# Second attention of a gated two-layer block on one core: scores in two PSUM banks, values in 32-column tiles, new orders

## The chip, the cores and the metric

One NeuronCore of a Trainium2 chip runs the whole program as one launch. The metric is device microseconds of an execution; the quoted time is the median of several executions. Engines are called TensorE (PE in rows, PEld its weight loads), VectorE (DVE), ScalarE (ACT), GpSimd (POOL) and SyncE (SP).

## The reference, cut to what matters

There are 16 batches of 256 tokens with 256 features, and a context of 120 rows for each batch.

```python
x = x + tanh(g_xattn[0]) * L0_xattn(layernorm(x), ctx, mask, ...)   # "A"
x = x + tanh(g_ffn[0])   * L0_ffn(layernorm(x), ...)                # "F", fp4-quantised, width 704
x = x + tanh(g_xattn[1]) * L1_xattn(layernorm(x), ctx, ctx, ...)    # "B"
x = x + tanh(g_ffn[1])   * L1_ffn(layernorm(x), ...)                # router "R" + experts "M"

# B: 16 heads of 16 features, all 120 context rows as keys and values
Q = (query @ Wq + bq); K = (key @ Wk + bk); V = (value @ Wv + bv)   # each split in 16 heads
attn = softmax(Q K^T / 4); ctx = attn @ V
return ctx @ Wo + bo
```

A is an attention of 4 heads of 64 features with one shared key and value head, rotary positions and a mask. R takes the two best of 8 experts per token (logits = x @ Wr + br). M runs the experts (width 1024) over the sorted tokens.

## The kernel before

**Two parts.** First a software pipeline over the 16 batches does A, F, B and the routing R, and splits the experts' weights in two fp16 parts (W). Then the expert phase M walks over tiles of sorted tokens; the change does not touch its code.

**Orders.** Each engine has a list in `ORDER` of stage/lag entries, which is worked through once in each step s, for batch s − lag. So in one steady step A of batch s, F of s − 1 (partly s − 2), and B and R of s − 3 (B's projections of s − 2) are interleaved on TensorE. A stage waits on semaphores for what it needs, so the order in a list decides what sits behind a wait. Steps run from s = −1 to 18; the steady ones take about 60 us.

**Numbers.** fp16 products are made of three matmuls (`three`, L1247 to L1249): high × high, low × high, high × low. Scores, transposes and values are fp32; an fp32 matmul that is no transpose shows as two records, each with a weight load of its own.

**B's rounds.** B has 8 rounds of 4 heads for each batch (2 halves `t` of 128 tokens × 4 rounds). Round k:
- B.s: TensorE writes scores of 4 heads (128 × 480) to `bank[3]` (L1319). It waits until the exponentials of round k − 1 have read that bank. VectorE takes the minimum of each head (L1008), ScalarE makes four exponentials to `b_ex[k % 2]` (L687).
- B.t: TensorE turns the four heads into `bank[4]` (L1332), ScalarE copies them to `b_pt` (L695).
- B.p: TensorE loads each head's turned probabilities as the stationary operand (120 × 128) and streams the head's values, 16 columns and one of ones (17 in all, L1343), into `bank[5]`. The 17th column is the sum of probabilities.
- After the last round of a half VectorE takes the reciprocal of the sums and multiplies (L1016, L1018).

After both halves B.ot turns the result (four transposes, L1359) into `bank[3]`, ScalarE copies the fp16 high part (L706), VectorE makes the low part (L972), and B.out multiplies by Wo, with the bias `bo` added by two one-row matmuls for each half (L1369, L1370). The key bias is also added by two one-row fp16 matmuls for each of four groups (L1431), the router's bias by one fp32 one-row matmul for each half (L1465).

**PSUM.** bank 0: A's turned input, half of A's queries, A's scores, A's turned output. bank 1: A's context, keys and values, turned probabilities, output. bank 2: the other half of A's rotary queries, then A's values. Bank 3, 4 and 5: B as above; B's queries use 3 and 5. Bank 5 also holds all of R, so B.q waits for `R.done`. Banks 6 and 7: F.

Of the kernel before, what the change touches and what calls it, by code (L numbers as in the profile page):

```python
# [34 lines left out]
QUAD = 4  # L35
WCH = 6
# [29 lines left out]
def gated_stack(nc, x, ctx, mask, g_x, g_f, rms_scale, q_w, kv_w, out_w, w_gate, w_up, w_down,  # L66
# [12 lines left out]
    with es:  # L79
# [25 lines left out]
        ones_h = sb("ones_h", [1, P], f16)  # L105
# [30 lines left out]
        bk_h = sb("bk_h", [1, 2, H1 * PITCH], f16)  # L136
        bvb = sb("bvb", [S, D])
        bo_h = sb("bo_h", [1, 2, D], f16)
        wr_s = sb("wr_s", [P, NK, NE])
        br_s = sb("br_s", [1, NE])  # L140
# [137 lines left out]
        class Signals:  # L278
# [12 lines left out]
         B.ot_mm, B.ot_hi, B.ot, B.out_mm, B.done, B.acc_out0, B.acc_out1) = (  # L291
            sem(f"b_{n}") for n in (
                "c_in0 c_in1 chain stats power rsqrt z zt ct zt_hi zt_lo ct_hi ct_lo q_mm k_mm q k v_mm v s_mm mn rd "
                "exp pt_mm pt pv_mm o ot_mm ot_hi ot out_mm done acc_out0 acc_out1").split())
# [22 lines left out]
        A.name, B.name = "A", "B"  # L317

# [31 lines left out]
        def over(ap, n):  # L350
# [7 lines left out]
            "SP": ("A.load/-1 B.out/3 B.load/0 W/0 R.rank/3").split(),  # L358
            "POOL": ("B.ln/2 R.ln/3 A.ln/-1 F.p0/1 W0/0 W1/0 F.p1/1 F.ln/0 W2/0 F.p/0 R.scatter/3").split(),
            "ACT": ("F.gu3/2 B.k/3 B.q/3 B.s0/3 B.s1/3 B.t0/3 F.ht0/2 B.s2/3 B.t1/3 B.t2/3 B.s3/3 F.ht1/2 A.s0/0 B.t3/3 "  # L360
                "B.s4/3 B.s5/3 B.t4/3 F.z/1 A.s1/0 A.t0/0 B.s6/3 B.t5/3 A.t1/0 B.s7/3 B.t6/3 B.t7/3 F.t/1 A.ot/0 B.ot/3 "
                "F.gu0/1 B.z/2 F.gu1/1 R.z/3 R.t/3 A.z/-1 B.ct/2 B.zt/2 F.gu2/1 A.t/-1 R.logit/3").split(),
# [291 lines left out]
        def _(act):  # L654
# [162 lines left out]
        def _(dve):  # L817
# [777 lines left out]
```

## Time and profile before

| | |
|---|---|
| median of 3 runs | 1848.67 us |
| fastest, slowest run | 1848.36, 1865.61 us |
| the profiled execution: its time | 1838.81 us |
| its span, first to last instruction | 1837.2 us |
| mean granted TensorE clock | 0.922 of full |

The profiled execution is 1.61 us longer than its span, and 9.86 us shorter than the median. In the profile's rows PE is a matmul, and its duration is not its distance to the next one: matmuls overlap, so the pace is read from one start to the next. A row of waits names the waiting engine and line, then what ended the wait.

### The profile page before, as it was taken

The page shows a single profiled execution, that of the slowest core. Times are in us where ns is not written, and L with a number is a line of the kernel's source. Part 1 is how long each engine was busy: PE and PEld are TensorE (multiplying, and loading weights), DVE is VectorE, ACT ScalarE, POOL GpSimd, SP SyncE. Part 2 cuts the span into 40 slices and gives each one's busy share as a digit, 9 for nine tenths or more (in the row PEclk, how much of TensorE's full clock was granted, in tenths as well). Part 3 has the DMA queues.
Part 4 walks back from the last instruction along what each step waited for, and adds up shares of the span by engine and source line. Part 5 has one row for each costly group of instructions (what it writes and reads, how often), then busy time and mean ns, then how long its engine had stood idle before and what let it go on. Part 6 is the DMA issues. An engine that isn't in the chain of part 4 may idle for free.

```text
span 1837.2 us, 35831 instructions
## 1 busy us (share of the span) xinstructions
PE 1540.0 (84%) x12221; PEld 1239.6 (67%) x12222; DVE 1121.2 (61%) x2782; ACT 886.8 (48%) x2169; POOL 591.9 (32%) x704
## 2 busy tenths in 40 slices
PE   2334899999998999899989877649999999999994
PEld 1223577667766767676766554438888888888884
DVE  4657678877787778787777552234444444444442
ACT  1111466656666656665655453214444544445542
POOL 0002324333434243334332421023443434434432
PEclk9557999999999999999999896569999999999998
DMA  5002211222022202221122000157213232232224
GB/s 172 11 0 78 81 57 37 92 92 84 10 92 92 91 9 87 92 93 43 51 84 84 7 7 12 48 160 239 39 32 100 34 103 34 33 101 34 29 34 114
DMA packets 63088, 123.60 MB, mean 67 GB/s; under 512 B 13890, under 2 KB 51899, under 8 KB 58811
## 3 DMA queue, kind: packets, MB, share of 16 engines
q1 hardware_dynamic: 45675, 102.75, 16.3%
q0 software_dynamic: 17312, 19.56, 6.6%
q8 instruction: 57, 0.93, 0.2%
q14 instruction: 44, 0.36, 0.1%
HBM read 78.63 MB, written 48.04 MB: 69 GB/s over the span
## 4 chain that ended last, share of the span: by engine, by line
PE 76%; DVE 9%; ACT 7%; issue 3%; DMA 2%; POOL 1%; SPq 0%; ACTq 0%; DVEq 0%; POOLq 0%
PE bank L1247 17%; PE bank L1249 16%; PE bank L1248 16%; PE bank L1319 9%; PE bank L1343 7%; PE bank L1332 3%; ACT b_ex L687 2%; DVE b_mn L1008 2%; ACT b_q L747 1%; PE bank L1359 1%; PE bank L1521 1%; ACT r_z L670 1%; PE bank L1467 1%; PE bank L1411 1%; PE bank L1431 1%
## 5 line engine op out<-in xcount | busy, mean ns | idle before, releaser
L1247 PE MATMUL bank<-split_room,wm 128*128 128x256 f16 x1152 | 314.9, 273 | 8.3 <-issue 6.9
L1249 PE MATMUL bank<-split_room,wm 128*128 128x256 f16 x1152 | 314.8, 273 | 0.0
L1248 PE MATMUL bank<-split_room,wm 128*128 128x256 f16 x1152 | 314.7, 273 | 0.0
L1224 DVE SCALAR_TENSOR_TENSOR split_room<-bank,b12e,split_room 128x256 f32<-128x256 f32 x288 | 138.3, 484 | 266.0 <-ACT split_room L798 258.2
L798 ACT ACTIVATE split_room<-bank,b12e 128x256 f32<-128x256 f32 x288 | 134.3, 470 | 196.0 <-PE bank L1249 192.6
L687 ACT ACTIVATE b_ex<-bank,b_mn 128x120 f32<-128x120 f32 x512 | 143.6, 373 | 117.5 <-DVE b_mn L1008 116.4
L1319 PE MATMUL bank<-b_k,b_q 128*128 128x480 f32 x256 | 140.8, 634 | 39.0 <-ACT b_ex L687 23.3
L1343 PEld LDWEIGHTS bank<-b_v,b_pt 120*128 120x128 f32 x1024 | 137.9, 204 | 36.0 <-issue 31.7
L643 POOL DMA_INDIRECT acc<-split_room,m_cur x72 | 115.3, 1602 | 131.7 <-ACT split_room L812 104.3
L1247 PE MATMUL bank<-wm,split_room 128*128 128x256 f16 x576 | 157.0, 273 | 0.0
L1249 PE MATMUL bank<-wm,split_room 128*128 128x256 f16 x576 | 157.0, 273 | 0.0
L1248 PE MATMUL bank<-wm,split_room 128*128 128x256 f16 x576 | 157.0, 273 | 0.0
L1008 DVE TENSOR_REDUCE b_mn<-bank 128x4 f32<-128x480 f32 x128 | 84.0, 656 | 95.1 <-PE bank L1319 91.8
L1343 PE MATMUL bank<-b_v,b_pt 120*128 120x17 f32 x1024 | 132.2, 265 | 0.9 <-DVE b_z L1018 0.9
L552 POOL TENSOR_TENSOR wm<-wm 128x704 f32<-128x704 f32 x32 | 53.5, 1672 | 245.8 <-DVE wm L1062 245.8
L1247 PEld LDWEIGHTS bank<-split_room,wm 128*128 128x128 f16 x1152 | 113.0, 98 | 23.8 <-issue 10.5
L806 ACT ACTIVATE split_room<-split_room 128x256 f16<-128x256 f32 x288 | 117.6, 408 | 19.8 <-DVE split_room L1224 18.0
L1249 PEld LDWEIGHTS bank<-split_room,wm 128*128 128x128 f16 x1152 | 113.0, 98 | 13.3
L1248 PEld LDWEIGHTS bank<-split_room,wm 128*128 128x128 f16 x1152 | 113.0, 98 | 13.2
L1235 DVE TENSOR_TENSOR split_room<-split_room 128x256 f16<-128x256 f32 x288 | 119.9, 416 | 2.2 <-ACT split_room L806 2.1
L695 ACT ACTIVATE b_pt<-bank 120x512 f32<-120x512 f32 x128 | 77.8, 608 | 74.1 <-PE bank L1332 74.0
L1332 PE MATMUL bank<-C,b_ex 128*120 128x128 f32 x512 | 83.8, 289 | 24.7 <-ACT b_pt L695 23.4
(358 smaller groups left out, 3859.7 us busy)
## 6 DMA issues: line engine op xcount, KB each, us to landing
split_room<-in_L_ffn_W SPq DMA_DIRECT2D x48, 512.0 KB, 8.4
wsplit<-split_room SPq DMA_DIRECT2D x16, 1536.0 KB, 6.5
wm<-wsplit SPq DMA_DIRECT2D x16, 1536.0 KB, 8.9
acc<-x SPq DMA_DIRECT2D x17, 256.0 KB, 2.1
xin<-in_x SPq DMA_DIRECT2D x16, 256.0 KB
rows<-r_row SPq DMA_DIRECT2D x16, 256.0 KB, 8.2
ct<-in_ctx SPq DMA_DIRECT2D x16, 120.0 KB
cb<-in_ctx SPq DMA_DIRECT2D x16, 120.0 KB, 2.1
```

Of the source, the lines that this page charges most:

```text
L687: last = act.activation(ex[:, k % 2, h], sb_[:, h * S:(h + 1) * S], ACT.Exp, bias=mn[:, k % 2, h:h + 1], scale=-1.0)
L798: act.activation(m_s[:, c % 2], bank[c % 4][:, 0:TILE], ACT.Silu, bias=b12e[:, p, 0, c:c + 1]).then_inc(M.silu, 1)
L806: act.activation(m_hh[:, 0, c], m_h[:, c % 3], ACT.Copy).then_inc(M.hi, 1)
L1008: dve.tensor_reduce(mn[:, k % 2], s4, AX.X, ALU.min).then_inc(G.mn, 1)
L1224: dve.scalar_tensor_tensor(m_h[:, c % 3], bank[c % 4][:, TILE:2 * TILE], b12e[:, p, 1, c:c + 1], m_s[:, c % 2], ALU.add, ALU.mult).then_in ...
L1235: dve.tensor_tensor(m_hh[:, 1, c], m_h[:, c % 3], m_hh[:, 0, c], ALU.subtract).then_inc(M.lo, 1)
L1247: pe.matmul(o, lh, rh, start=start, stop=False)
L1248: pe.matmul(o, ll, rh, start=False, stop=False)
L1249: return pe.matmul(o, lh, rl, start=False, stop=stop)
L1319: last = pe.matmul(sbk[:, at:at + side * S], q[:, c, t * P:(t + 1) * P], kk[:, c] if G is B else kk[:, :, :], start=G is B, stop=G is B or ...
L1332: last = pe.transpose(tbk[0:S, j * P:(j + 1) * P], ex[:, k % 2, j], ident)
L1343: last = pe.matmul(pbk[:, h * (width + 1):(h + 1) * (width + 1)], pt[:, k % 2, h - h0], v[:, h] if G is B else v[:, :], start=True, stop=True)
```

## The change

1. **A in two banks.** A.q is cut in A.q0 and A.q1 (a pair of heads each), each with its plain and its half-swapped product side by side, in bank 0 and in bank 1. The rotary stage on VectorE is cut in A.rk (keys and values), A.r0 and A.r1. A.q1 waits for `A.v`, since bank 1 held keys and values. A's values go to bank 0 (after the last exponentials) and bank 1. Bank 2 becomes free.
2. **B's scores in two banks by turns**, 3 and 2: B.s of round k waits for the exponentials of round k − 2. The exponentials now wait for the transposes of round k − 2, and for the reciprocal that reads the sums of the batch before. B's queries are made in banks 3 and 2, and B.q no longer waits for `R.done`; B.p of round 0 does.
3. **B's values stationary.** In B.p the values of a head (120 rows × 32 columns, 16 of them zeros) are the stationary operand, in one of four 32-column tiles, and the head's turned probabilities (120 × 128, fp32) stream. Two rounds accumulate in the same tiles. The result comes out turned already, 128 features × 128 tokens twice.
4. **Sums by accumulation.** Each exponential has an `accum_out`, the sum of its row. B.rx on VectorE takes the reciprocal of the 16 sums and spreads it over 256 columns (`b_rx`); TensorE turns that by two transposes at the end of B.p of each half, next to the values in bank 5. ScalarE copies it to SBUF (B.r), VectorE multiplies (B.p), ScalarE makes the high part (B.o), VectorE the low part (B.o). The stages B.ot, its four transposes among them, are gone, and B.out needs only the half it works on. The last transposes wait for B.rx.
5. **Biases.** bo and bk lie as high part in row 0 and low part in row 32 of a 33-row operand, and one matmul adds both. The router's bias is added by VectorE.
6. **Orders.** All five lists are new. On ScalarE R.logit (an exponential) moves from before the last gate activation F.gu3 to behind it. On TensorE R.rank moves behind B.q, F.ht0 moves from the end of a step to the next one's start, and B's rounds from t0 on belong to the next step. On SyncE the weights (W) come before B.out and B.load; on GpSimd W0 and W1 come before F.p0, and B.ln and R.ln are at the end. In preparation there are 8 DMAs more, and some memsets are larger.

```diff
-            "PE": ("F.ht1/2 A.s0/0 B.t3/3 B.s4/3 B.p2/3 A.s1/0 A.t0/0 B.s5/3 B.t4/3 F.d0/2 B.s6/3 B.p3/3 F.d1/2 B.p4/3 "
-                "B.t5/3 B.s7/3 A.t1/0 A.p0/0 B.t6/3 B.p5/3 A.p1/0 B.t7/3 F.t/1 B.p6/3 B.p7/3 A.ot/0 B.ot/3 F.gu0/1 "
-                "B.out/3 A.out/0 F.gu1/1 B.ct/2 B.zt/2 R.t/3 F.gu2/1 R.logit/3 A.t/-1 F.gu3/1 R.rank/3 B.k/2 B.q/2 "
-                "A.kv/-1 B.s0/2 B.v/2 A.q/-1 B.s1/2 B.t0/2 F.ht0/1 B.s2/2 B.p0/2 B.t1/2 B.t2/2 B.s3/2 B.p1/2").split(),
+            "SP": ("A.load/-1 W/0 B.out/3 B.load/0 R.rank/3").split(),
+            "POOL": ("A.ln/-1 W0/0 W1/0 F.p0/1 F.p1/1 F.ln/0 R.scatter/3 F.p/0 W2/0 B.ln/1 R.ln/2").split(),
+            "ACT": ("F.ht0/2 B.t2/3 B.s3/3 A.s0/0 F.ht1/2 B.t3/3 B.s4/3 B.s5/3 B.t4/3 B.s6/3 B.r3/3 F.z/1 A.s1/0 A.t0/0 "
+                "B.t5/3 A.t1/0 B.o0/3 B.s7/3 B.t6/3 F.t/1 B.t7/3 B.r7/3 B.o1/3 A.ot/0 F.gu0/1 B.z/2 F.gu1/1 R.z/3 R.t/3 "
+                "B.ct/2 A.z/-1 F.gu2/1 B.zt/2 A.t/-1 F.gu3/1 R.logit/3 B.k/2 B.q/2 B.s0/2 B.s1/2 B.t0/2 B.s2/2 B.t1/2").split(),
+            "DVE": ("A.rk/0 B.v/3 B.s1/3 F.q1b/2 B.s2/3 F.q1c/2 A.r0/0 A.r1/0 B.s3/3 F.ht0/2 A.s0/0 B.s4/3 F.ht1/2 B.s5/3 "
+                "F.ln/1 B.s6/3 B.rx0/3 W0/1 A.s1/0 B.p3/3 F.q/1 B.o0/3 B.s7/3 F.d1/2 W1/1 A.p0/0 A.p1/0 B.rx1/3 F.t/1 "
+                "W2/1 B.p7/3 B.ln/2 B.o1/3 A.ot/0 B.out/3 F.gu0/1 R.ln/3 A.out/0 A.ln/-1 F.gu1/1 F.q0a/1 B.ct/2 R.t/3 "
+                "F.gu2/1 B.zt/2 R.logit/3 A.t/-1 F.gu3/1 F.q0b/1 F.q1a/1 F.q0c/1 R.rank/3 B.s0/2").split(),
+            "PE": ("B.t0/3 B.s2/3 A.q1/0 B.p0/3 B.t1/3 F.ht0/2 B.t2/3 B.s3/3 B.p1/3 A.s0/0 F.ht1/2 B.t3/3 B.s4/3 B.p2/3 "
+                "B.s5/3 A.s1/0 B.t4/3 B.s6/3 A.t0/0 B.p3/3 F.d0/2 B.p4/3 B.t5/3 B.s7/3 A.t1/0 F.d1/2 B.t6/3 A.p0/0 A.p1/0 "
+                "F.t/1 B.p5/3 B.t7/3 A.ot/0 B.p6/3 B.p7/3 F.gu0/1 B.out/3 A.out/0 F.gu1/1 B.ct/2 B.zt/2 R.t/3 F.gu2/1 "
+                "A.t/-1 R.logit/3 F.gu3/1 B.k/2 B.q/2 R.rank/3 A.kv/-1 B.s0/2 B.v/2 B.s1/2 A.q0/-1").split(),
...
                         for h in range(QUAD):
-                            last = act.activation(ex[:, k % 2, h], sb_[:, h * S:(h + 1) * S], ACT.Exp,
-                                                  bias=mn[:, k % 2, h:h + 1], scale=-1.0)
+                            at = head_of(k % per, h)
+                            last = act.activation(ex[:, k % 2, h], sb_[:, h * S:(h + 1) * S], ACT.Exp, bias=mn[:, k % 2, h:h + 1], scale=-1.0,
+                                                  accum_out=b_sum[:, k // per, at:at + 1] if G is B else None)
...
+            def b_rx_(t):
+                def stage(b, p):
+                    dve.wait_ge(B.exp, b * RB + (t + 1) * (RB // NT))
+                    dve.reciprocal(b_rd[:, t], b_sum[:, t]).then_inc(B.rd, 1)
+                    if t or not isinstance(b, int) or b >= 1:
+                        held(dve, B.pv_mm, b * NT + t)
+                    dve.wait_ge(B.rd, b * NT + t + 1)
+                    dve.tensor_copy(b_rx[:, :, :].rearrange("p k (h d) -> p (k h) d", d=K1), over(b_rd[:, t], K1)).then_inc(B.rx, 1)
+                return stage
...
-                        else:
-                            pe.wait_ge(G.exp, b * n + k)
+                        elif k >= len(sbks):
+                            pe.wait_ge(G.exp, b * n + k + 1 - len(sbks))
+                        sbk = sbks[k % len(sbks)]
...
+                            r, c = k % per, k % per % 2
+                            for j in range(QUAD):
+                                at = r // 2 * (H1 // 2 * PITCH) + (4 * c + j) * PITCH
+                                last = pe.matmul(pbk[PITCH * j:PITCH * (j + 1), c * P:(c + 1) * P], v[:, at:at + PITCH], pt[:, k % 2, j],
+                                                 start=r == 0, stop=r == per - 1)
+                            if r == per - 1:
+                                pe.wait_ge(B.rx, b * NT + t + 1)
+                                for i in range(NK):
+                                    last = pe.transpose(pbk[:, D + i * P:D + (i + 1) * P], b_rx[:, i], ident)
...
-                    pe.matmul(o, ones_f[:, :], br_s[:, :], start=True, stop=False)
                     for k in range(NK):
-                        last = pe.matmul(o, r_zt[:, k, t * P:(t + 1) * P], wr_s[:, k], start=False, stop=k == NK - 1)
+                        last = pe.matmul(o, r_zt[:, k, t * P:(t + 1) * P], wr_s[:, k], start=k == 0, stop=k == NK - 1)
```

## Rows read from the trace of the kernel before

**Rows 1.** The page: busy time by engine, and the granted clock in 40 slices.

```profile
PE 1540.0 (84%) x12221; PEld 1239.6 (67%) x12222; DVE 1121.2 (61%) x2782; ACT 886.8 (48%) x2169; POOL 591.9 (32%) x704
...
PEclk9557999999999999999999896569999999999998
```

**Rows 2.** Stages: us, busy and count of each engine, clock, DMA share, GB/s.

```profile
461.60:521.40 59.80, 54.74 (x424) 41.77 (x422) 47.82 (x122) 37.52 (x92) 21.68 (x25) 1.00 0.20 69
521.40:582.50 61.10, 56.21 (x422) 42.19 (x420) 47.74 (x122) 37.43 (x92) 21.67 (x25) 0.97 0.21 72
1006.70:1069.80 63.10, 51.87 (x321) 36.97 (x321) 36.99 (x93) 31.94 (x75) 22.07 (x22) 0.86 0.03 10
1131.90:1176.00 44.10, 32.47 (x122) 23.52 (x122) 7.68 (x14) 15.52 (x45) 0.21 (x1) 0.63 0.00 1
1222.00:1837.00 615.00, 584.77 (x5472) 523.31 (x5470) 282.56 (x684) 280.59 (x697) 240.28 (x292) 0.98 0.31 73
```

**Rows 3.** TensorE's waits from 461.6 to 521.4: total us, times, longest.

```profile
PE bank L1332 <- ACT b_pt L695: 1.3, 1, 1.3
PE bank L1457 <- ACT r_z L670: 1.1, 1, 1.1
PE bank L1319 <- ACT b_q L747: 0.8, 1, 0.8
PE bank L1319 <- ACT b_ex L687: 0.8, 1, 0.8
PE bank L1359 <- DVE b_z L1018: 0.6, 1, 0.6
PE bank L1369 <- DVE b_zt L972: 0.4, 1, 0.4
```

**Rows 4.** Timeline of TensorE around the bias matmuls.

```profile
501.74 0.28 PE L1369 MATMUL bank<-bo_h,ones_h 1*128 1x256 f16 x1 [0.44 <-DVE b_zt L972]
501.86 0.27 PE L1370 MATMUL bank<-bo_h,ones_h 1*128 1x256 f16 x1
502.06 0.28 PE L1247 MATMUL bank<-wo,b_zt 128*128 128x256 f16 x1
502.17 0.27 PE L1248 MATMUL bank<-wo,b_zt 128*128 128x256 f16 x1
...
511.57 0.38 PE L1465 MATMUL bank<-br_s,ones_f 1*128 1x8 f32 x2
511.88 0.61 PE L1467 MATMUL bank<-wr_s,r_zt 128*128 128x8 f32 x4
```

**Rows 5.** Timeline of TensorE from 530 us: start, duration, operation.

```profile
530.64 1.07 PE L1319 MATMUL bank<-b_k,b_q 128*128 128x480 f32 x2 [1.04 <-ACT b_ex L687]
531.55 0.96 PE L1343 MATMUL bank<-b_v,b_pt 120*128 120x17 f32 x8
532.36 0.63 PE L1332 MATMUL bank<-C,b_ex 128*120 128x128 f32 x4
```

**Rows 6.** Timeline of VectorE: a minimum, rotary, and the second attention's division.

```profile
531.75 0.66 DVE L1008 TENSOR_REDUCE b_mn<-bank 128x4 f32<-128x480 f32 x1 [0.68 <-PE bank L1319]
...
533.32 0.67 DVE L987 TENSOR_TENSOR a_t<-bank,C 128x512 f32<-128x512 f32 x1
...
547.57 0.24 DVE L1016 RECIPROCAL b_rd<-bank 128x16 f32<-128x16 f32 x1
547.85 0.42 DVE L1018 TENSOR_TENSOR b_z<-bank,b_rd 128x256 f32<-128x256 f32 x1
```

**Rows 7.** Timeline of ScalarE: table loads, and a round of exponentials.

```profile
516.16 0.20 ACT L759 ACTIVATE r_e<-r_d 128x2 f32<-128x2 f32 x1
...
524.84 1.28 ACT L687 ACT_TABLE_LOAD   x1 [1.93 <-DVE b_mn L1008]
526.14 1.11 ACT L687 ACTIVATE b_ex<-bank,b_mn 128x120 f32<-128x120 f32 x4
```

**Rows 8.** Timeline of TensorE at the last batch's output.

```profile
1176.12 0.39 PE L1369 MATMUL bank<-bo_h,ones_h 1*128 1x256 f16 x1 [1.50 <-DVE b_zt L972]
```

More of the change, by code:

```diff
@@ L668, in stage @@
                         held(act, R.free, b + 2)
+                    if G is B and (not isinstance(b, int) or b >= 1):
+                        act.wait_ge(B.ot, b * NT)
                     for t in range(NT):
@@ L698, in rounds @@
                 return by_round(G, n, s=exps, t=turned)
-            ra = rounds(A, RA, a_ex, bank[0], a_mn, a_pt, bank[1])
-            rb = rounds(B, RB, b_ex, bank[3], b_mn, b_pt, bank[4])
+            ra = rounds(A, RA, a_ex, bank[0:1], a_mn, a_pt, bank[1])
+            rb = rounds(B, RB, b_ex, (bank[3], bank[2]), b_mn, b_pt, bank[4])
             def out_t(G, ot, bk):
@@ L999, in a_rotary, with stage, rounds @@
                 last.then_inc(A.k, 1)
-            def rounds(G, n, sbk, pbk, mn, rd, o, heads, width):
+            def a_rotary(c):
+                def stage(b, p):
+                    ca.go_on(b)
+                    dve.wait_ge(A.q_mm, b * 2 + c + 1)
+                    ca.link(dve.tensor_tensor(a_t1[:, c], bank[c][:, 0:T], C[:, C_CQ:C_CQ + T], ALU.mult))
+                    ca.link(dve.tensor_tensor(a_t2[:, c], bank[c][:, T:2 * T], C[:, C_SQ:C_SQ + T], ALU.mult))
+                    ca.wait()
+                    dve.tensor_tensor(a_q[:, c], a_t1[:, c], a_t2[:, c], ALU.add).then_inc(A.q, 1)
+                return stage
+            def rounds(G, n, sbks, pbks, mn, rd, o, heads, width):
                 per = n // NT
@@ L1339, in stage @@
                         pe.wait_ge(G.pt, b * n + k + 1)
-                        if t >= 1 and k % per == 0:
-                            pe.wait_ge(G.o, b * NT + t)
-                        for h in range(h0, h0 + QUAD):
-                            last = pe.matmul(pbk[:, h * (width + 1):(h + 1) * (width + 1)], pt[:, k % 2, h - h0],
-                                             v[:, h] if G is B else v[:, :], start=True, stop=True)
+                        pbk = pbks[t]
+                        if G is A and t == 0:
+                            pe.wait_ge(A.exp, b * n + n)
+                        if G is B and k == 0:
+                            pe.wait_ge(R.done, b + 1)
+                        if G is B and t >= 1 and k % per == 0:
+                            pe.wait_ge(G.o, b * NT + t)
+                        if G is A:
+                            for h in range(h0, h0 + QUAD):
+                                last = pe.matmul(pbk[:, h * (width + 1):(h + 1) * (width + 1)], pt[:, k % 2, h - h0],
+                                                 v[:, :], start=True, stop=True)
+                        else:
+                            r, c = k % per, k % per % 2
[7 more added lines that the diff above has]
+                                    last = pe.transpose(pbk[:, D + i * P:D + (i + 1) * P], b_rx[:, i], ident)
                         if k % per == per - 1:
@@ L1368, in stage @@
                         if bias is not None:
[L1369 to L1370 removed]
+                            pe.matmul(o, ones_h[:, :], bias[:, :], start=True, stop=False)
+                            pe.wait_ge(G.ot, b * NT + t + 1)
                         for k in range(NK):
@@ L1429, in b_k_ @@
                 for c in range(QUAD):
-                    for i in range(2):
-                        pe.matmul(bank[4][:, c * S:(c + 1) * S], bk_h[:, i, c * P:(c + 1) * P], ones_h[:, 0:S], start=i == 0, stop=False)
+                    pe.matmul(bank[4][:, c * S:(c + 1) * S], bk_h[:, c * P:(c + 1) * P], ones_h[:, 0:S], start=True, stop=False)
                     for k in range(NK):
```

165 lines of the change are left out of this document (98 added, 67 removed), and 3 rows, old and new, of the table ORDER.

## The prediction

> **What bounds the kernel now.** I read the page first: TensorE is busy 84% of the span, VectorE 61%, ScalarE 48% [rows 1]. The reader is to see that this is an average over two phases. In the digits of the granted clock the pipeline over batches stands at 9 (full speed) from the fifth slice to about the twenty-second, then falls to 6 and 5 before the expert phase brings it back [rows 1]. The table by stage gives sizes [rows 2]: a steady step takes 59.8 us, of which TensorE is busy 54.7, VectorE 47.8, ScalarE 37.5; one of the steps at 0.97 of the clock takes 61.1. The step at 1006.7, when A has run out, still takes 63.1 us at a clock of 0.86; the last B rounds take 44.1 us at 0.63; the experts 615.0 us, which the change leaves alone. So 1222 us can move, and in the steady part TensorE sets the pace: its work plus its waits. The view of waits of one step lists six, 1.3, 1.1, 0.8, 0.8, 0.6 and 0.4, together 5.0 us [rows 3]. TensorE's work is then 54.8 us, which agrees with its busy time. A change can help by work taken off TensorE or by waits that go; nothing else counts in the steady part.
>
> **The work on TensorE.**
> - *Router bias.* From the bias matmul's start to the next group is 0.31 us [rows 4], twice a step: −0.62.
> - *Output bias.* Two one-row matmuls start 0.12 apart [rows 4]; one of them goes in each half: −0.24. The key bias is half as wide (120 columns for 256), so 0.055 each, four times: −0.22.
> - *Transposes.* B.ot's four go, four of the reciprocals come, of the same shape: 0.
> - *Values.* Before, a round took from 531.55 to 532.36, 0.81 us [rows 5], eight weight loads of 128 columns with nearly nothing streamed. After, a round has four heads of two passes over 128 columns. The price of a pass: scores of 480 columns take 0.91 us in two passes (530.64 to 531.55 [rows 5]), so 0.455 × 128/480 = 0.12 us. No row shows column tiles at work together, so I bound it. Eight passes one after the other: 0.97 us. All four tiles side by side: two passes, 0.24. To either I add two changes of the tile shape. The only rows near it are those at the one-row bias: from it to the full array the starts are 0.20 apart where the next is 0.11 [rows 4], so about 0.09 a change, 0.18 a round. Range: 0.42 to 1.15 us a round, against 0.81. I take a value between: if the passes keep their order, the second pass of a head must wait for the first in its tile but can run with the next head's first, five pass times for eight: 0.60 + 0.18 = 0.78. So −0.03 × 8 rounds = −0.24 a step; ends −3.1 and +2.7.
>
> Sum of the work: −0.62 − 0.24 − 0.22 − 0.24 = −1.3 us a step.
>
> The Trainium skill's page "TensorEngine Tiling (Array Packing)", section "Theoretical Speedup", allows up to four times for columns of 32, but "Key Properties" says that a change of mode drains the array. By the first alone values would cost about what the lower end has; the second speaks against the change, and the wider start distance at the one-row bias [rows 4] looks like such a drain, though it is a row tile and no run here shows a column one.
>
> **The waits on TensorE.** I went through the new list of each engine with the durations of the rows: a round of scores 0.9 us [rows 5], a minimum 0.66 [rows 6], four exponentials 1.11 [rows 7].
> - *Waits that go.* The scores' wait for the exponentials (0.8, L1319 ← b_ex [rows 3]) goes with the second bank. The waits for B.z and B.zt (0.6 and 0.4 [rows 3]) go with B.ot: what follows the last values is ScalarE copy, VectorE multiply 0.42 [rows 6], high part, low part, about 1.8 us with hand-overs, behind a whole gate matmul group and the first half of B.out. −1.8 us.
> - *Waits that shrink.* B.t2 on the copy of t1 (1.3 [rows 3]) gets F.ht0 as cover, but now depends on the minimum of round 2, which stands behind a quantisation piece on VectorE: I leave 0.6, −0.7. B.s0's wait for B.q (0.8) gets R.rank as cover: −0.3. R.t's wait for R.z (1.1) has the same chain in both lists and stays.
> - *Waits that come.* A.s0 now stands earlier on TensorE, while VectorE first has a quantisation piece and then both rotary stages: six operations over 256 columns at the 0.42 of the multiply [rows 6] are 2.5 us where three over 512 were 2.0 (0.67 each [rows 6]): +0.9. The transposes at the end of B.p3 wait for B.rx, behind the minimum of round 6 on VectorE: reciprocal 0.24, spread about 0.4: +0.5. What is queued behind that is F.d0 and all after. B.t4 and B.p0, with less other work ahead of them: +0.5 and +0.3. Sum +2.2. Behind B.t4's wait stand B.s6 and the values.
> - *ScalarE's table loads.* Each is 1.28 us; one stands directly before the first exponentials of a batch [rows 7]. With R.logit behind F.gu3 the table of the exponentials stays, two loads for four. This takes 1.28 us out of the chain to B.t0 and is the reason that I add no wait there, although B.s0's minimum now stands behind R.rank's chain.
> - *Accumulated sums.* No row shows an exponential with accumulation. Bounds: free, or an extra instruction for each, at the 0.20 us of the smallest activation [rows 7], 0.8 a round. I take 0.05 for each, 0.2 a round, as the chain's instructions overlap; about two of the gates above feel it: +0.4.
>
> Waits: −1.8 − 1.0 + 2.2 + 0.4 = −0.2. With the work, −1.5 us a step. My walk ends more favourably where TensorE is later than its partners (its work is nowhere less than the rows say), and a wait that I count twice along one chain is paid once: four waits that come hang on one VectorE queue. I take 1.0 us off for that, estimated: −2.5 us a step, 57.3 for 59.8. VectorE then has 47.8 + about 1.3 (rotary 0.5, spreads 0.8) = 49.1 of 57.3.
>
> **The ends.** From 222.7 to 1006.7 us there are 13 steps: −33. The last 170 us before the experts are chains, not work. There the second bank lets scores run ahead, fewer table loads count in full, and B.ot's latency (a wait of 1.5 us on it at the end [rows 8], and its own transposes) goes: about −3 us for each of the three: −9. The preparation has eight DMAs more on SyncE, ahead of the first weights, and larger memsets; VectorE's preparation of B comes at step 2, long after: +1, between 0 and +4. W ahead of B.out on SyncE delays a store by four issues, which nothing needs for a step; W0 and W1 ahead of F.p0 on GpSimd run in time in which it stood idle. 0 for both. Sum −41: 1838.8 − 41 = 1797.8 for a profiled execution. The median stood 9.86 above the profiled one, so 1807.7; forecast 1808 us.
>
> **The rivals.**
> 1. *Column tiles side by side.* Then a round costs 0.42, −3.1 a step for −0.24: 2.9 × 16 = 46 us more: 1762. For it: the heads write four different groups of partitions. Against: fp32 needs two passes per head in order, and eight short instructions with a change of shape on both sides. The Trainium skill's page "TensorE: Matmul & The Clock Gate", section "Part 3: Packing small matmuls", reports 2.38 times for three column tiles; nothing in this trace bears on it.
> 2. *Column tiles one by one.* 1.15 for 0.78, 0.37 × 8 × 16 = 47 us: 1855, no change.
> 3. *The accumulators gate (slower).* If the sum costs an instruction of 0.20 to 0.28 us for each exponential, a round on ScalarE grows by 0.8 to 1.1 us, and ScalarE has 8 rounds in a step: +7 to +9 on 37.5 − 2.6. It is still under the step, but B.t0, B.p0, B.t2, B.t3, B.t4 and B.rx each stand close behind a round of exponentials. Six gates × 0.8 = 4.8, less 0.4 already counted: +4.4 × 16 = 70: 1878. It decides from about 0.15 us for each sum. For it: the waits of before behind ScalarE are half of all [rows 3]. Against: between gates the chain has slack.
> 4. *VectorE takes over.* It has 49 of 57; should the waits on it not overlap, my 1.0 us goes and the three ends give nothing: 1848.7 − 16 × 1.3 = 1828.
>
> **How the numbers follow.** A few runs of this kernel tell no change from one of 1%, 18.5 us. Chances: forecast (1785 to 1830) 0.42, rival 4 at its edge included in "faster" at 0.10; rival 1 0.20; rival 2 0.15; rival 3 0.13. Faster by over 1% (below 1830): 0.42 × 0.97 + 0.10 × 0.6 + 0.20 = 0.67; rival 2 lies within 1% for the most: same 0.18; slower 0.15. The range must reach rival 1 nearly and rival 2: 1755 to 1858, which leaves out rival 3 and some of rival 1, 0.2 in all.
>
> **What the profile would show.** Step length by the table of stages: 57.3. TensorE's rows at B.p: from the first of four heads to the next stage 0.78. Waits: no L1319 ← b_ex for B; A.s0 on the rotary 0.9; the reciprocal's transposes 0.5. Table loads 2 for 4 a step. The exponentials: 1.11 against 1.3. I am wrong if new waits on VectorE's queue at the start of a step exceed 2 us, if the clock falls below 0.97 in steady steps, or if a record of its own follows each exponential.

## The result, and the profile after

| | before | after |
|---|---|---|
| median of the runs | 1848.51 us (1834.79 to 1865.61) | 1753.41 us (1750.41 to 1754.71) |
| profiled execution: time, span | 1838.8, 1837.2 | 1752.59, 1751.0 |
| mean granted clock | 0.922 | 0.933 |

The changed kernel takes 0.951 of the time before (95% interval 0.945 to 0.956). The forecast was 1808 with a range from 1755: the direction was right, the gain of 95 us is more than twice the 41 that the sum gave, and the time lies just below the range.

The page's busy times, its granted clock in 40 slices and the head of its chain that ended last, of the kernel after, answer to [rows 1]:

```profile
PE 1444.2 (82%) x12061; PEld 1110.5 (63%) x12062; DVE 1150.0 (66%) x2878; ACT 910.7 (52%) x2701; POOL 595.4 (34%) x704
...
PEclk9556799999999999999999988599999999999997
...
PE 51%; DVE 28%; ACT 7%; issue 6%; POOL 5%; DMA 1%; SPq 0%; DVEq 0%; ACTq 0%; POOLq 0%
```

The head of the same chain in the kernel before:

```profile
PE 76%; DVE 9%; ACT 7%; issue 3%; DMA 2%; POOL 1%; SPq 0%; ACTq 0%; DVEq 0%; POOLq 0%
```

TensorE lost 96 us of busy time, VectorE gained 29. The two slices at 8 and the one at 5 after the pipeline stand where before had 8, 9, 6, 5, 6. VectorE's part of the chain rose from 9% to 28%.

Stages of the kernel after by windows (us, busy and count of each engine, clock, DMA share, GB/s): a steady step, the three stretches after A has run out, the experts. They answer to [rows 2].

```profile
446.50:502.70 56.20, 50.13 (x413) 34.63 (x411) 49.50 (x128) 38.71 (x125) 22.21 (x25) 1.00 0.23 76
952.20:1009.20 57.00, 42.99 (x311) 26.79 (x311) 39.33 (x97) 33.05 (x109) 18.44 (x20) 0.91 0.03 10
1009.20:1060.50 51.30, 36.94 (x259) 24.10 (x259) 23.21 (x68) 27.20 (x100) 12.29 (x14) 0.83 0.04 12
1060.50:1094.90 34.40, 22.04 (x136) 10.70 (x136) 9.80 (x29) 18.94 (x80) 3.91 (x4) 0.87 0.01 1
1136.00:1751.00 615.00, 584.76 (x5466) 523.05 (x5464) 282.41 (x684) 280.89 (x697) 241.38 (x292) 0.98 0.30 72
```

The two stretches of before whose like [rows 2] doesn't show, cut at the same events (the last one ends where VectorE begins to add B's output to the rows):

```profile
1069.80:1131.90 62.10, 44.52 (x269) 32.52 (x269) 23.28 (x67) 24.84 (x65) 16.35 (x18) 0.78 0.03 9
1131.90:1180.20 48.30, 36.39 (x138) 25.23 (x138) 7.74 (x14) 15.52 (x45) 0.21 (x1) 0.62 0.00 1
```

A step is the distance between two evictions of B's queries (`b_q`) on ScalarE. With it the 86.2 us of the span fall into three parts. The first eviction is at 222.6 us in one trace and at 222.7 in the other: the preparation cost nothing. The next 13 steps took 784.1 us and take 729.5: −54.6, where I had −33. From there to the first expert matmul it was 215.1 us and is 182.3: −32.8, where I had −9. The experts are 1.1 us longer. Not all of before's thirteen steps are at full clock; the next paragraph takes one that is.

In the steady step the two numbers that I had set up as work and waits can be read directly. TensorE's busy time went from 54.74 [rows 2] to 50.13: −4.6. Its waits are these (us in total, times, longest), against 5.0 in [rows 3]:

```profile
PE bank L1401 <- ACT b_ex L710: 1.7, 1, 1.7
PE bank L1541 <- ACT r_z L685: 1.1, 1, 1.1
PE bank L1384 <- DVE a_t L1037: 0.9, 1, 0.9
PE bank L1388 <- ACT b_q L782: 0.7, 1, 0.7
PE bank L1470 <- POOL f_z L567: 0.6, 1, 0.6
PE bank L1429 <- DVE b_rx L1073: 0.4, 1, 0.4
PE bank L1497 <- DVE f_ht L1159: 0.3, 1, 0.3
PE bank L1401 <- ACT b_pt L718: 0.2, 1, 0.2
```

They sum to 5.9, so +0.9. Work and waits give −3.7, the step −3.6. The reader should see that the waits did not shrink at all: they changed their places. In a step at full clock all of the gain is work.

Most of that work is the values. TensorE's timeline around two places of B.p in the kernel after, to be read against the middle row of [rows 5]:

```profile
480.08 0.43 PE L1424 MATMUL bank<-b_pt,b_v 120*32 120x128 f32 x8
480.43 0.65 PE L1401 MATMUL bank<-C,b_ex 128*120 128x128 f32 x4
...
481.45 0.83 PE L1424 MATMUL bank<-b_pt,b_v 120*32 120x128 f32 x16
482.21 0.44 PE L1429 MATMUL bank<-C,b_rx 128*128 128x128 f32 x2
```

From start to the next start one round takes 0.35 us, and two take 0.76, where one took 0.81: 0.45 × 8 = −3.6 a step. The trace's single records show how: in the round at 480.08 four of the eight matmuls start within 0.02 us, and the other four, again within 0.02 us, begin 0.13 us after the first. Before, the eight of a round start 0.11 apart. With the −1.1 of the bias terms that is −4.7, and the busy time shows −4.6.

### The profile page after: what moved, and what is told of

Its sections match the earlier page's. It is cut to its first block, busy times and chain, and to the rows that moved or that the text cites. A ratio compares the mean times of both kernels' runs of the same rounds, so it can differ in the third digit from the quotient of the medians.

```text
span 1751.0 us, 36348 instructions
## 1 busy us (share of the span) xinstructions
PE 1444.2 (82%) x12061; PEld 1110.5 (63%) x12062; DVE 1150.0 (66%) x2878; ACT 910.7 (52%) x2701; POOL 595.4 (34%) x704
## 4 chain that ended last, share of the span: by engine, by line
PE 51%; DVE 28%; ACT 7%; issue 6%; POOL 5%; DMA 1%; SPq 0%; DVEq 0%; ACTq 0%; POOLq 0%
PE bank L1312 13%; PE bank L1314 13%; PE bank L1313 13%; PE bank L1388 3%; DVE b_mn L1047 2%; ACT b_ex L710 2%; POOL f_z L567 2%; PE bank L1401 2%; DVE wm L1125 1%; POOL f_z L565 1%; DVE wm L1117 1%; DVE r_pick L1219 1%; PE bank L1424 1%; DVE a_t L1037 1%; POOL slots L595 1%
## 5 line engine op out<-in xcount | busy, mean ns | idle before, releaser
L710 ACT ACTIVATE b_ex<-bank,b_mn 128x120 f32<-128x120 f32 x512 | 177.4, 360 | 130.0 <-DVE b_mn L1047 121.1
L1388 PE MATMUL bank<-b_k,b_q 128*128 128x480 f32 x256 | 129.1, 586 | 13.9 <-ACT b_q L782 13.9
L1047 DVE TENSOR_REDUCE b_mn<-bank 128x4 f32<-128x480 f32 x128 | 83.3, 651 | 59.8 <-PE bank L1388 53.7
L710 ACT ACTIVATION_READ_ACCUMULATOR b_ex<-bank,b_mn 128x1 f32 x512 | 104.4, 204 | 0.0
L1401 PEld LDWEIGHTS bank<-C,b_ex 128*120 128x120 f32 x512 | 56.1, 140 | 68.4 <-ACT b_ex L710 45.3
L625 POOL DMA_INDIRECT split_room<-rows,m_next x76 | 75.0, 987 | 43.2 <-POOL m_next L622 31.8
```

The lines of the kernel that those rows point to most:

```text
L710: last = act.activation(ex[:, k % 2, h], sb_[:, h * S:(h + 1) * S], ACT.Exp, bias=mn[:, k % 2, h:h + 1], scale=-1.0, accum_out=b_sum[:, k ...
L1047: dve.tensor_reduce(mn[:, k % 2], s4, AX.X, ALU.min).then_inc(G.mn, 1)
L1388: last = pe.matmul(sbk[:, at:at + side * S], q[:, c, t * P:(t + 1) * P], kk[:, c] if G is B else kk[:, :, :], start=G is B, stop=G is B or ...
L1401: last = pe.transpose(tbk[0:S, j * P:(j + 1) * P], ex[:, k % 2, j], ident)
```

## The experiments

After this result my theory was: values in column tiles run side by side (rival 1) and that is the steady gain; the two banks keep TensorE from standing still, and so keep its clock, in the ends. Rivals: the orders alone carry the gain; the sums still cost something; a wait on VectorE can be had back by a better order. "Step" is the mean of the first 12 steps, "rest" the time from the last of them to the first expert matmul, both from one profile; "before" is the median of the kernel before on the same chip.

| kernel | median, us | ratio to before (95%) | before | step | rest |
|---|---|---|---|---|---|
| before | 1848.5 | | | 60.0 | 279.0 |
| after | 1753.4 | 0.951 (0.945 to 0.956) | 1848.5 | 56.2 | 238.0 |
| one_tile | 1783.3 | 0.963 (0.959 to 0.967) | 1854.5 | 58.5 | 245.1 |
| one_bank | 1891.9 | 1.022 (1.017 to 1.026) | 1854.5 | 64.6 | 275.3 |
| no_sums | 1770.8 | 0.956 (0.952 to 0.960) | 1854.5 | 56.8 | |
| old_orders | 1875.1 | 1.013 (1.008 to 1.018) | 1854.5 | 64.3 | 259.3 |
| one_bank_busy | 1852.9 | 1.013 (1.008 to 1.018) | 1828.1 | 62.1 | 265.6 |
| tables_back | 1812.7 | 0.991 (0.987 to 0.995) | 1828.1 | 59.9 | 254.1 |
| rank_later | 1754.2 | 0.959 (0.955 to 0.963) | 1828.1 | 56.2 | |
| before_bias | 1835.7 | 1.003 (1.000 to 1.007) | 1828.1 | 60.0 | |
| before_busy | 1851.3 | 1.000 (0.997 to 1.004) | 1850.3 | | |
| after_busy | 1766.8 | 0.957 (0.951 to 0.963) | 1850.3 | | |
| v_first | 1757.2 | 0.952 (0.946 to 0.958) | 1850.3 | 56.2 | |
| rotary_first | 1783.7 | 0.973 (0.970 to 0.976) | 1829.9 | 58.0 | |

The kernel before differs by 1.4% from chip to chip (1828 to 1854), and its gain with it: rank_later, within 1 us of after, is 74 us under the before of its chip, where after is 95 under its own. After itself ran on one chip only. On three others rank_later (1754.2), v_first (1757.2) and no_sums (1770.8, of which 16.4 are longer experts, as told below) stand within 4 us of it, so I compare variants of after by their own medians and steps, and use the ratio for the sign. The steps of before come from a profile on the first chip; beside a variant from another chip they are a weaker measure.

**one_tile: the four heads of a round in one column tile.** Each head gets its round's tile; four heads overwrite two column ranges in turn, so the values are not those of the reference; count and shape of the instructions stay.

```
-  last = pe.matmul(pbk[PITCH * j:PITCH * (j + 1), c * P:(c + 1) * P], v[:, at:at + PITCH], pt[:, k % 2, j],
-                   start=r == 0, stop=r == per - 1)
+  last = pe.matmul(pbk[PITCH * r:PITCH * (r + 1), j % 2 * P:(j % 2 + 1) * P], v[:, at:at + PITCH], pt[:, k % 2, j],
+                   start=j == 0, stop=j == QUAD - 1)
```

> The kernel after, but the four heads of a round of B.p all go to one 32-column tile (round r to tile r), so that they can't run side by side; the tile shape, the 32-column weight loads and all orders stay (the values of B come out wrong, so its result is not the reference's). Theory, overlap: the after-rows show a round of B.p in 0.35 us from start to start where eight passes of 128 columns one after the other would be 8 x 0.11 = 0.9 us; so +0.5 x 8 x 16 = +64 us, about 1817 us. Rival, weight loads: the gain in B.p came from the loads (32 columns for 128), and tiles don't matter: within 10 us of 1753.

TensorE's timeline in one_tile, the same places as above:

```profile
488.52 1.06 PE L1424 MATMUL bank<-b_pt,b_v 120*32 120x128 f32 x8
489.51 0.65 PE L1401 MATMUL bank<-C,b_ex 128*120 128x128 f32 x4
...
490.76 1.53 PE L1424 MATMUL bank<-b_pt,b_v 120*32 120x128 f32 x16
492.22 0.44 PE L1429 MATMUL bank<-C,b_rx 128*128 128x128 f32 x2
```

A round takes 0.99, or 0.73 where two stand together (these two lie in two different tiles), for 0.35 and 0.38: the tiles do run side by side, both passes of fp32 included, and the 32-column weight loads, which one_tile has too, don't explain it. 0.99 is my upper end without the change of shape (0.97). TensorE's busy time in a step rises by 4.5 us (50.1 to 54.6), as the rounds add (six times 0.64 and twice 0.35), but the kernel lost only 2.3 us a step: the waits for A's rotary, for `f_z`, for `b_rx` and for `f_ht` are gone, 2.2 us of them, because TensorE now comes later than VectorE. The theory on tiles holds; its price in time is reduced by waits that were behind it. The time it expected, 1817, was 34 us too high for the same reason.

**one_bank: B's scores in one bank again.**

```
-            rb = rounds(B, RB, b_ex, (bank[3], bank[2]), b_mn, b_pt, bank[4])
+            rb = rounds(B, RB, b_ex, (bank[3],), b_mn, b_pt, bank[4])
```

(and so in the two other engines' programs)

> The kernel after, but B's scores use bank 3 alone, so that round k waits for the exponentials of round k-1 again; all orders stay. Theory, overlap of tiles carries the steady steps and the second bank mainly the ends: +1 us a step and +10 at the ends, about 1780 us. Rival, the second bank carries the change: +3 us a step and more, over 1805 us.

It is slower than the kernel before, and 112 us above what the theory expected. The largest wait of a step from 482 us, then TensorE's timeline behind it, and the window of that stretch:

```profile
PE bank L1388 <- ACT b_ex L710: 5.8, 2, 3.8
```

```profile
486.82 1.97 PE L1388 MATMUL bank<-b_k,b_q 128*128 128x480 f32 x2 [3.78 <-ACT b_ex L710]
488.59 0.42 PE L1312 MATMUL bank<-a_zt,wqa 128*128 128x256 f16 x1
488.80 0.42 PE L1313 MATMUL bank<-a_zt,wqa 128*128 128x256 f16 x1
```

```profile
486.80:492.00 5.20, 5.17 (x18) 3.38 (x19) 1.99 (x3) 1.48 (x8) 0.00 (x0) 0.50 0.00 0
482.00:547.00 65.00, 54.89 (x410) 37.38 (x409) 49.86 (x130) 39.11 (x124) 21.69 (x27) 0.92 0.20 65
```

In the list of after, only B.v stands between B.s0 and B.s1; with one bank B.s1 needs the exponentials of round 0 to be done, 3.8 us. Behind this wait the granted clock is 0.50: fp16 matmuls of 256 columns start 0.21 apart, 1.2 GHz, where they start 0.11 apart in after, 2.4 GHz. The step has 5.8 − 1.7 = 4.1 us more waits, and 54.9 for 50.1 = 4.8 us more busy time for the same instructions. So half of the 8.4 us is a wait and half the clock that it takes away.

**one_bank_busy: matmuls in front of these waits.** one_bank, with matmuls into the bank that nothing else uses:

```
                         elif k >= len(sbks):
+                            if G is B and k in (1, 5):
+                                for _ in range(24 if k == 1 else 10):
+                                    pe.matmul(bank[2][:, 0:D], wo1[:, 0, 0, 0:P], wo1[:, 0, 1], start=True, stop=True)
```

> The kernel with scores in one bank (1891.9 us), and on TensorE, right before the waits of B.s1 and B.s5 for the exponentials, 24 and 10 extra fp16 matmuls of 256 columns (0.11 us each) into bank 2, whose results nobody reads. Nothing is taken away and both waits end when they did. Theory, the clock: the wait of 3.8 us before B.s1 is followed by 5 us of rows at half speed (matmuls 0.21 apart for 0.11), so work put into the wait keeps the clock: about 2.5 us a step less, 1850 us. Rival: the clock there follows from something else: 1892 us or more by what the extra work costs.

A step of it by windows:

```profile
482.00:544.00 62.00, 54.40 (x443) 37.83 (x442) 49.98 (x127) 38.79 (x124) 21.95 (x25) 1.00 0.21 69
```

Against the row of one_bank above TensorE has 33 more records and 0.5 us less busy time, and the clock is at 1.00. The 34 added matmuls are 3.7 us of work at full clock and stand in the waits, so the clock gave back about 4.2 us a step, near the 4.8 above; the step is 2.5 us shorter. That the clock is a cost of its own is shown. The kernel's median is 39 us lower, but the two ran on different chips; by the ratios to before it is 0.8%, some 16 us.

**no_sums: exponentials without accumulation.** The sums are a constant, so B's softmax is not normalised.

```
-  last = act.activation(ex[:, k % 2, h], sb_[:, h * S:(h + 1) * S], ACT.Exp, bias=mn[:, k % 2, h:h + 1], scale=-1.0,
-                        accum_out=b_sum[:, k // per, at:at + 1] if G is B else None)
+  last = act.activation(ex[:, k % 2, h], sb_[:, h * S:(h + 1) * S], ACT.Exp, bias=mn[:, k % 2, h:h + 1], scale=-1.0)
```

> The kernel after without accum_out: the exponentials don't sum, the sums are a constant set once (the softmax of B is not normalised rightly). The rows after show the exponentials 0.34 apart and a read of the accumulator for each, where they were 0.25 apart before: 0.37 us a round on ScalarE. Theory: only the wait before B.t0 and the last chain of rounds feel it, -0.4 us a step, -10 us in all, about 1743. Rival (the prediction's third): six gates in a step feel it, -2.2 us a step, -35 us or more.

ScalarE's timeline in after shows what was taken away:

```profile
399.94 0.36 ACT L710 ACTIVATE b_ex<-bank,b_mn 128x120 f32<-128x120 f32 x1
400.20 0.19 ACT L710 ACTIVATION_READ_ACCUMULATOR b_ex<-bank,b_mn 128x1 f32 x1
400.29 0.35 ACT L710 ACTIVATE b_ex<-bank,b_mn 128x120 f32<-128x120 f32 x1
```

Each exponential is followed by a record of 0.20 us, which is rival 3's instruction, but the exponentials start 0.34 apart for 0.25: 0.09 more each, 0.37 a round. Without it nothing is gained: the start of the experts is 1138.6 against 1134.5, and the wait before B.t0 is 1.6 for 1.7. It now ends on VectorE's `b_v` and not on the exponentials, so VectorE's queue hides what the sums cost there. The median is 17 us longer because the phase of the experts takes 632.9 us for 616.5; wrong values of B send the rows to the experts otherwise, which I take for the reason. It says nothing on the sums. Rival 3 fell: the instruction is there and costs nothing in this kernel.

**old_orders: the changed code with the lists of before.** B.r, B.rx and A.rk, which before doesn't have, are put in where their inputs are there. TensorE's list begins as before's:

```
-            "PE": ("B.t0/3 B.s2/3 A.q1/0 B.p0/3 B.t1/3 F.ht0/2 B.t2/3 B.s3/3 B.p1/3 A.s0/0 F.ht1/2 B.t3/3 B.s4/3 B.p2/3 "
+            "PE": ("F.ht1/2 A.s0/0 B.t3/3 B.s4/3 B.p2/3 A.s1/0 A.t0/0 B.s5/3 B.t4/3 F.d0/2 B.s6/3 B.p3/3 F.d1/2 B.p4/3 "
...
```

> The kernel after with the five order lists of the kernel before, the new stages put in where their partners stood (B.rx behind the minimum of its half's round 6 or behind A.p1, B.r and B.o at B.ot's and B.p's places, A.rk at the end of a step on VectorE). Theory, the operations carry the change: work on TensorE is 4.5 us a step less whatever the order, so most of the gain stays, 1775 to 1800 us. Rival, the orders carry it: 1830 us or more.

1.3% slower than before, though TensorE has 4.6 us less to do in a step. Its largest waits from 472 to 538 us:

```profile
PE bank L1401 <- ACT b_pt L718: 3.2, 2, 1.7
PE bank L1401 <- ACT b_ex L710: 2.8, 1, 2.8
PE bank L1312 <- DVE wm L1148: 1.7, 2, 1.0
```

With the smaller ones they are 11.0 us for 5.9, and the clock is 0.90 to 0.95 in the steps but the first. The theory's 1775 to 1800 missed, the rival's 1830 or more holds: work taken from TensorE counts only if the lists let the partners follow.

**tables_back: one entry of ScalarE's list.**

```
-                "... A.t/-1 F.gu3/1 R.logit/3 B.k/2 B.q/2 B.s0/2 B.s1/2 B.t0/2 B.s2/2 B.t1/2").split(),
+                "... A.t/-1 R.logit/3 F.gu3/1 B.k/2 B.q/2 B.s0/2 B.s1/2 B.t0/2 B.s2/2 B.t1/2").split(),
```

> The kernel after with R.logit on ScalarE back in front of the last gate activation, as in the kernel before: four table loads a step for two. Theory: the load of 1.28 us stands again between the minimum and the first exponential, before which TensorE waits already: +1.2 us a step, about 1772. Rival: ScalarE is idle there for 4 us and takes the load meanwhile: within 3 us of 1753.

The table loads on ScalarE from 480 to 540 us, and TensorE's largest wait there:

```profile
501.00 1.28 ACT L751 ACT_TABLE_LOAD   x1
513.16 1.28 ACT L794 ACT_TABLE_LOAD   x1 [0.74 <-DVE r_d L1198]
514.67 1.28 ACT L751 ACT_TABLE_LOAD   x1
526.10 1.28 ACT L710 ACT_TABLE_LOAD   x1 [5.53 <-DVE b_mn L1047]
```

```profile
PE bank L1401 <- ACT b_ex L710: 4.5, 1, 4.5
```

Four loads for two. The last stands in the chain to B.t0, whose wait grows from 1.7 to 4.5. As A.s0's wait is gone, the waits of a step grow only by 1.8 in sum; the step grows by 3.7, with TensorE busy for some 2 us more, and its clock is 0.94 to 0.97. Without this one entry the kernel is 59 us slower, also against rank_later on the same chip. I had expected 19: again a load was priced by its duration and not by what a longer wait does to the clock.

**rank_later, v_first, rotary_first: the waits on VectorE.** The first two put R.rank's chain behind B.s0, and behind B.v too; the third puts A's rotary before a piece of the experts' quantisation, and F.ht1 two entries later.

```
-  rank_later:   F.q0c/1 R.rank/3 B.s0/2      v_first: A.rk/0 B.v/3 B.s1/3           rotary_first: F.q1c/2 A.r0/0 A.r1/0 B.s3/3
+                F.q0c/1 B.s0/2 R.rank/3               A.rk/0 B.s1/3                               A.r0/0 A.r1/0 F.q1c/2 B.s3/3
+                                                      F.q0c/1 B.s0/2 B.v/2 R.rank/3
```

> The kernel after with one entry moved on VectorE: R.rank behind B.s0 instead of before it. In the rows after, R.rank's chain takes 4.1 us there (it took 1.7 before), because two of its operations last until a GpSimd operation that runs beside them ends (1.59 and 1.16 us), and the minimum of round 0 stands behind it; TensorE then waits 1.7 us before B.t0. Theory: that wait goes, about 1.2 us a step, 1735 us. Rival: the keys' stage A.rk and the minimum of round 1 come as much later, and the wait moves to A.q1 or B.t1: within 5 us of 1753.

> The kernel after with VectorE's order B.s0, B.v, R.rank, A.rk where it is R.rank, B.s0, A.rk, B.v. With R.rank alone behind B.s0 the wait before B.t0 stayed at 1.5 us and only changed its releaser, to B.v. Theory: with both ahead TensorE waits at most 0.3 us there, and A.q1 takes 0.5 of it: -1.0 us a step, 1738 us. Rival, VectorE's queue as a whole is the bound up to A.s0 (its wait 0.9 for the rotary stage): what goes at B.t0 comes at A.s0, within 5 us of 1753.

> The kernel after with both rotary stages on VectorE ahead of the quantisation piece F.q1c, and F.ht1, which needs that piece, two entries later on TensorE and ScalarE. In the rows after, A.s0 waits 0.9 us for the last rotary addition, which itself lasts 0.83 and 1.34 us (two operations) beside a GpSimd operation that F.q1c has released. Two runs showed that what goes at B.t0 comes back before A.s0. Theory, VectorE's queue up to the rotary stage is the bound of this stretch: the wait goes and the additions last 0.4 each: -1 us a step, 1738 us. Rival, the later F.q1c gives it back at F.ht1 or at B.t3: within 5 us of 1753.

TensorE's largest wait in the step from 446.5 in rank_later and in v_first, and the three largest of a step in rotary_first:

```profile
PE bank L1401 <- DVE b_v L1180: 1.5, 1, 1.5
```

```profile
PE bank L1424 <- ACT b_pt L718: 1.5, 1, 1.5
```

```profile
PE bank L1401 <- ACT b_ex L710: 2.6, 2, 1.9
PE bank L1429 <- DVE b_rx L1073: 2.0, 1, 2.0
PE bank L1470 <- POOL f_z L567: 1.3, 1, 1.3
```

The wait keeps its size (1.7, 1.5, 1.5) and changes its name: at B.t0 on the exponentials, at B.t0 on `b_v`, at B.p0 on `b_pt`. Neither list moves the time (steps 56.2). In rotary_first the wait for A's rotary is gone (0.9), and three others grow by 3 us: 1.9 us a step slower. So these waits behave as one backlog on VectorE. None of the three lists beats after.

**before_bias: one part alone in the kernel before.** The router's bias is added by VectorE at the eviction.

```
-  cr.link(dve.tensor_copy(r_lg[:, :, :], ...))
+  dve.wait_ge(misc_in, 64)
+  cr.link(dve.tensor_tensor(r_lg[:, :, :], ..., br_s[:, :].unsqueeze(1).to_broadcast([P, NT, NE]), ALU.add))
...
-                    pe.matmul(o, ones_f[:, :], br_s[:, :], start=True, stop=False)
```

> The kernel before with one part of the change alone: the router's bias added by VectorE, two fp32 one-row matmuls a step less on TensorE. Theory (work off TensorE counts in full): 0.31 us each, -0.62 a step, -10 us, 0.5%. Rival: R.t's and the later waits take it up, 0.

Nothing that can be told from zero (0 to 12 us slower). Its steps at full clock are 59.1 to 59.7 us for 59.0 to 60.1, with TensorE busy 54.0 for 54.7, as the 0.62 says. But among the first twelve stand two of 62.3 at a clock of 0.95 and two of 60.8 at 0.97, and the mean is 60.0, as before. Alone, such a saving was not seen in the time.

**before_busy and after_busy: matmuls in front of the waits in the last two batches.** Ten matmuls ahead of each wait of B.s and six ahead of B.t's in the kernel before, six and ten in the kernel after (shown), from batch 14 on.

```
+                        if G is B and b >= NB - 2:
...
+                            for _ in range(6):
+                                pe.matmul(bank[0][:, 0:D], wo1[:, 0, 0, 0:P], wo1[:, 0, 1], start=True, stop=True)
```

> The kernel before, and for the last two batches alone 6 extra fp16 matmuls (256 columns, 0.11 us each) before the waits of each B.t and 10 before those of each B.s, into bank 0, which A no longer uses; nobody reads them. The two last stages before had TensorE's clock at 0.78 and 0.62 and scores of 1.6 us from start to start for 0.8. Theory, the clock prices the ends: with the waits filled the rounds run at full speed, and these stages lose 10 us or more, although each batch has 14 us more work at full clock: 10 us under the kernel before run beside it, in the profile 8 us or more from the last but two B.q to the experts. Rival, the chain alone prices them: slower by what the extra work adds, 0 to +15 us.

> The kernel after with extra matmuls of the same kind, 10 before each B.t's waits and 6 before each B.s's, for the last two batches alone. There the waits (10 us in the last stage) are shorter and the clock higher (0.83 and 0.87) than before. Theory, the clock: -3 us, 1750. Rival, the work adds: +5 us.

In before the last batch fell from 89.9 to 83.4 us and the one ahead of it rose from 62.1 to 67.9: nothing. Up to the last output, the stretch that was 48.3 us at a clock of 0.62, it is 42.4 at 0.96: there the clock gave back more than the added matmuls took, and one batch earlier it did not. After was 13 us slower, mostly in the step 58.7 for 51.3. Where the waits are short, or the rest full, such matmuls are work like other work.

What the clock alone is worth in the ends is better seen in the stretch of before_busy that has no added matmul yet. It is the same code as the step at 1006.7 in [rows 2], 63.1 us at 0.86, in another execution, on another chip:

```profile
1027.90:1086.00 58.10, 45.58 (x324) 33.15 (x325) 37.00 (x93) 31.88 (x75) 21.36 (x22) 0.97 0.03 10
```

The same work took 5.0 us less at 0.97. That the clock is a large part of the time in the ends is thus shown; what in the changed kernel raised it is not.

## Why the prediction was wrong

- **Values on TensorE: the step that failed.** "If the passes keep their order, the second pass of a head must wait for the first in its tile but can run with the next head's first": 0.78 us a round. Measured 0.35 to 0.38, below my lower end of 0.42, since the two changes of shape cost at most 0.35 − 0.24 = 0.11 and not 0.18 (one_tile's 0.99 over eight passes of 0.12 leaves 0.02). What I took for a condition, that the second pass of a head runs beside the next head's first only, did not bind: four heads run side by side. This is rival 1: −3.6 a step for −0.24, and its 1762 us was the nearest to the result. The Trainium skill's "TensorEngine Tiling (Array Packing)" has both rules, up to four times under "Theoretical Speedup" and the drain at a change of mode under "Key Properties"; one_tile against after gives 0.99 to 0.35, 2.8 times, and 0.73 to 0.38, 1.9 times (one_tile's two rounds there use two tiles), so the first bore the result and the second hardly showed. I had given weight to the drain from a row tile of one partition [rows 4].
- **Other work.** −1.1 for the biases agrees with −4.6 of busy time, less the values.
- **Waits.** −0.2 forecast, less 1.0 for overlap; +0.9 measured. A.s0 came at 0.9 as forecast, `b_rx` at 0.4 for 0.5, B.q at 0.7, R.z unchanged at 1.1. Not foreseen were 1.7 at B.t0 and 0.6 at `f_z`. At B.t0 I had excused R.rank's chain by the table load that goes. With less work on TensorE the backlog of VectorE shows instead, which was rival 4's mechanism inside rival 1's case. Over 13 steps the error on the values is 44 us too little gain and the one on the waits 27 too much; that they cancel in part is luck.
- **Steady steps.** −2.5 forecast, −3.6 measured at a full clock; 13 steps gave −54.6 for −33, of which 8.2 in the thirteenth alone, whose clock was 0.92 before and is 1.00 after. Three more steps of before stood at 0.97; all of after's are at 1.00.
- **The ends.** −9 forecast, −32.8 measured: the second largest error. The step that failed here is "chains, not work", which leaves out the granted clock, though [rows 2] had shown 0.86 and 0.63 there. In the three stretches TensorE's busy time fell by 8.9, 7.6 and 14.4 us at nearly the same counts (321 to 311, 269 to 259, 138 to 136), while the clock rose from 0.86, 0.78 and 0.62 to 0.91, 0.83 and 0.87. That is 31 of the 32.8 us, of which less work, at a steady step's 4.7, is 14 at the most; the rest is clock. The waits did not shrink here either: length less busy time is 11.2, 17.6 and 11.9 us before and 14.0, 14.4 and 12.4 after, 40.7 in sum in both kernels. From the twelfth step on, one_bank gives back 37 us of 41, old_orders 21, tables_back 16, one_tile 7, so the gain needs the second bank above all; by what it raised the clock, with as much waiting as before, stays open.
- **From the profile to the median.** I carried over the 9.86 us between them. After has 0.8, which is 9 of the 54 us that the forecast is off.
- **The second bank.** I credited it with 0.8 us a step, the wait in [rows 3]. With the new lists its loss costs 8.4, half of it clock. The parts are no sum: tiles 2.3, bank 8.4, orders 8.2 a step for a total of 3.85. With either of bank and lists taken back, the kernel is slower than before; the second bank alone in the kernel before was not run.
- **Table loads.** Two fewer, as foreseen, but "the reason that I add no wait there" understates 3.7 us a step.
- **Rival 3.** Right about the instruction, wrong about the cost: the gates had slack.
- **Nothing forecast, nothing found:** preparation 0 for +1, experts +1.1, the moved DMAs not in the waits of TensorE.

## What to carry to other kernels

Matmuls whose output needs 32 partitions are worth putting into four column tiles in fp32 too: price eight passes as little more than two pass times (0.35 us here, for an estimated 0.24), and the whole round as what the free VectorE and ScalarE can follow. Price a wait on TensorE by its length and by the granted clock of the rows behind it as well, where the same instructions can take twice as long, as behind the 3.8 us here; a buffer or a table load that looks like 1 us can then be 4 to 8 a step. Before moving an entry to hide a wait, ask whose queue is full: where one engine has a backlog, the wait only changes its name.

## What the runs showed of the hardware

- **The clock falls behind one wait of 3.8 us.** The stretch behind it ran at 0.50 for at least 5.2 us; waits of up to 1.7 us in after left the step at 1.00. 34 matmuls without use in each step brought one_bank's clock back to 1.00 and its step from 64.6 to 62.1 us.
- **It also falls without such a wait.** A step of before_busy ahead of any added matmul, so in the code of before, has the waits of [rows 3] to the tenth, none over 1.3 us, and still stands at 0.51 over the 10 us from 782.9 us on; it takes 64.6 us for 59.8:

```profile
770.40:835.00 64.60, 59.53 (x422) 44.92 (x419) 47.69 (x122) 37.69 (x91) 21.74 (x25) 0.92 0.19 67
```

  So the length of the longest wait does not settle the clock of a step, and the kernel before loses such time in some steps and executions and not in others.
- **VectorE stands still beside GpSimd.** VectorE's timeline, and GpSimd's, in one step of after:

```profile
447.22 0.17 DVE L1217 TENSOR_TENSOR r_cnt<-bank,r_cnt 128x8 f32<-128x8 f32 x1
447.30 1.67 DVE L1219 TENSOR_TENSOR r_pick<-r_m,r_sl 128x16 f32<-128x16 f32 x2
...
449.11 1.23 DVE L1225 TENSOR_SCALAR r_w<-r_e,g_inv 128x2 f32<-128x2 f32 x1
```

```profile
447.18 1.67 POOL L565 TENSOR_TENSOR wm<-wm 128x704 f32<-128x704 f32 x1 [6.67 <-DVE wm L1125]
448.93 1.39 POOL L567 TENSOR_TENSOR wm<-wm,f_hs 128x704 f32<-128x704 f32 x1
```

  The same two lines in a step of before, where GpSimd is at rest:

```profile
516.56 0.25 DVE L1154 TENSOR_TENSOR r_pick<-r_m,r_sl 128x16 f32<-128x16 f32 x2
516.95 0.22 DVE L1160 TENSOR_SCALAR r_w<-r_e,g_inv 128x2 f32<-128x2 f32 x1
```

  Operations over 16 and 2 columns last until GpSimd's is over. The one that reads a PSUM bank doesn't. A's rotary meets the same 10 us later: its additions take 1.34 and 0.83 us where the products from the bank take 0.42. So some 2.4 us of R.rank's 4.1 us chain, and 1.3 of the rotary, are this. The Trainium skill's "SBUF — State Buffer", section "SBUF: two separate sides", says that GpSimd and VectorE, with two SBUF inputs among other cases, lock a shared pair of ports for a whole instruction; the row of `r_pick`, two SBUF inputs, agrees, 1.67 beside 1.67 us. `r_w` has one SBUF tensor and one number for each partition, and stood still all the same. No run moved the dequantisation away from GpSimd, so what the kernel would gain isn't shown.
- **An accumulated sum is a record of its own,** 0.20 us on ScalarE, but adds only 0.09 us to the distance of two exponentials, 0.34 for 0.25.
